# Layer 1 and layer 2 of an expert network on TensorE: one by one, or in pairs

## What is computed

```python
# block 1: gated recurrence along the sequence
g = sigmoid(norm(x) @ Wg.T + bg);  h = scan(h * (1 - g) + g * norm(x))
x = x + norm(h @ Wo.T + bo)
# block 2: top-1 of 8 experts, 320 places each, 2-layer networks 256 -> 1024 -> 256
eid = argmax(softmax(norm(x) @ router_w + router_b)); rank = place in the expert's queue
y = relu(buf @ w1 + b1) @ w2 + b2                       # for tokens with rank < 320
yov = relu(norm(x) @ ow1 + ob1) @ ow2 + ob2             # for all the others
x = x + norm(y or yov)
```

## Time and profile before

| | us |
|---|---|
| median of 3 runs | 1175.66 (1174.62 to 1176.27) |
| profiled execution | 1174.9 |
| its span | 1173.2 |
| PE busy | 1142.9 (97%) |
| DVE busy | 995.6 (85%) |
| ACT busy | 743.6 (63%) |
| POOL busy | 691.4 (59%) |

### The profile page before, as it was taken

One profiled execution on the slowest core, in us unless ns is written; L12 is line 12 of the kernel. 1 busy time (PEld: TensorE's weight loads), 2 busy tenths in 40 slices (PEclk: granted clock), 3 DMA queues, 4 the chain that ended last, 5 costly groups with the idle time before them and its releaser, 6 DMA issues.

```text
span 1173.2 us, 24398 instructions
## 1 busy us (share of the span) xinstructions
PE 1142.9 (97%) x7539; PEld 1018.6 (87%) x7539; DVE 995.6 (85%) x2737; ACT 743.6 (63%) x1379; POOL 691.4 (59%) x792
## 2 busy tenths in 40 slices
PE   7789999999999999999999999999999999999996
PEld 4578889888898888898888888889988888899996
DVE  6868888888889898988888888888898987778885
ACT  5356666566666666666656665666666667678783
POOL 4447667566665656566666665666656664414544
PEclk9999999999999999999999999999999999999998
DMA  9131111111111111110100111111111100245430
GB/s 262 37 100 55 37 51 48 43 38 36 36 36 36 36 36 36 36 36 18 36 23 31 36 36 36 36 36 36 36 36 36 36 18 19 86 141 182 147 132 34
DMA packets 59428, 65.09 MB, mean 55 GB/s; under 512 B 7835, under 2 KB 55629, under 8 KB 59268
## 3 DMA queue, kind: packets, MB, share of 16 engines
q1 hardware_dynamic: 52228, 59.36, 15.6%
q0 software_dynamic: 7168, 5.34, 1.5%
HBM read 40.19 MB, written 38.76 MB: 67 GB/s over the span
## 4 chain that ended last, share of the span: by engine, by line
PE 89%; DVE 4%; POOL 3%; ACT 2%; issue 2%; DMA 0%; DVEq 0%; POOLq 0%; ACTq 0%
PE psY L1426 12%; PE psY L1429 11%; PE psY L1428 11%; PE psH L1320 11%; PE psH L1322 11%; PE psH L1321 10%; PE psA L1320 5%; PE psA L1321 5%; PE psA L1322 5%; PE psT L1376 3%; PE psT L1333 2%; DVE st L858 1%; PE psT L1389 1%; PE psT L1391 1%; POOL rstd L399 1%
## 5 line engine op out<-in xcount | busy, mean ns | idle before, releaser
L620 ACT ACTIVATE hid<-psH,biasT 128x512 f32<-128x512 f32 (+1 forms) x312 | 202.7, 650 | 217.4 <-PE psH L1322 216.4
L1426 PE MATMUL psY<-W_hi,hid_hi 128*128 128x256 f32 x1168 | 336.6, 288 | 0.8 <-DVE hid_lo L1011 0.8
L1429 PE MATMUL psY<-W_hi,hid_lo 128*128 128x256 f32 x1168 | 329.6, 282 | 0.0
L1428 PE MATMUL psY<-W_lo,hid_hi 128*128 128x256 f32 x1168 | 328.9, 282 | 0.0
L399 POOL TENSOR_TENSOR rstd<-veps,mhalf 128x4 f32<-128x4 f32 (+2 forms) x103 | 142.0, 1379 | 169.1 <-DVE nmean L870 169.1
L1011 DVE TENSOR_TENSOR hid_lo<-hid,hid_hi 128x512 fp32r<-128x512 f32 (+1 forms) x308 | 201.0, 664 | 44.4 <-ACT hid_hi L625 39.3
L1320 PE MATMUL psH<-xfT_hi,W_hi 128*128 128x512 f32 (+1 forms) x624 | 235.4, 377 | 0.3 <-ACT hid L620 0.2
L1322 PE MATMUL psH<-xfT_hi,W_lo 128*128 128x512 f32 (+1 forms) x624 | 235.5, 377 | 0.0
L1321 PE MATMUL psH<-xfT_lo,W_hi 128*128 128x512 f32 (+1 forms) x624 | 234.6, 376 | 0.0
L1426 PEld LDWEIGHTS psY<-W_hi,hid_hi 128*128 128x128 f32 x1168 | 220.0, 188 | 10.8 <-DVE hid_lo L1011 1.9
L1428 PEld LDWEIGHTS psY<-W_lo,hid_hi 128*128 128x128 f32 x1168 | 220.2, 189 | 6.4
(11 more groups left out here) (172 smaller groups left out, 2181.9 us busy)
## 6 DMA issues: line engine op xcount, KB each, us to landing
xin<-L_attn_x SPq DMA_DIRECT2D x32, 512.0 KB, 3.5
stage<-L_ffn_w SPq DMA_DIRECT2D x16, 1024.0 KB, 5.6
out<-outt SPq DMA_DIRECT2D x31, 512.0 KB, 2.8
xbuf<-zrow SPq DMA_DIRECT2D x1, 2590.0 KB, 15.8
xin<-xbuf SPq DMA_DIRECT2D x8, 259.0 KB, 5.0
stage<-L_ffn_ow SPq DMA_DIRECT2D x2, 1024.0 KB, 8.0
xbuf<-x,idx POOLq DMA_INDIRECT x128
b_b<-L_ffn_b SPq DMA_DIRECT2D x1, 1024.0 KB, 6.4
```

The lines of the kernel that those rows point to most:

```text
L620: act.activation(hid[j % 2][:, at:n], psH[:, j % 2, at:n], ACT.Relu, bias=bias).then_inc(s_hid, 1)
L1426: pe.matmul(dst, hi, w[0][:, j, :], start=(j == 0 and (tail or t % 2 == 0)), stop=False, skip_group_check=True)
L1428: pe.matmul(dst, hi, w[1][:, j, :], start=False, stop=False, skip_group_check=True)
L1429: last = pe.matmul(dst, lo_, w[0][:, j, :], start=False, stop=(j == HC - 1), skip_group_check=True)
```

## The change

Parts stand in pairs. In a steady step the order behind `project` is now `layer1(2)`, `layer1(3)`, `transposes0(far)`, `rank(now)`, `layer2(0)`, `layer2(1)`, `layer1(4)`, `layer1(5)`, `layer2(2)`, `layer2(3)`, `gate(far)`, `layer1(6)`, `layer1(7)`, `layer2(4)`, `layer2(5)`, `transposes1(nxt)`, `layer2(6)`, `layer2(7)`. In an expert: `layer1(0)` to `layer1(3)`, `layer2(0)`, `layer2(1)`, and so on by two, with `transposes1(nxt)` behind `layer2(5)` instead of ahead of it. The number of instructions, their sizes and the programs of the other engines are the same.

```diff
-                for j in range(2, HC):
+                for j in range(2, HC, 2):
                     if run:
                         layer1(now, j, GT, W1[1])
+                        layer1(now, j + 1, GT, W1[1])
                         if j == 2:
                             pe.wait_ge(s_y, cnt(now, 2, 0))
-                    if j == 3 and ahead:
+                    if j == 2 and ahead:
                         transposes0(far)
                     if run:
-                        if j == (3 if up else 2):
+                        if j == 2:
                             rank(now)
                         layer2(now, j - 2, TG, W2[1])
-                    if j == 5 and ahead:
+                        layer2(now, j - 1, TG, W2[1])
+                    if j == 4 and ahead:
                         gate(far)
...
-                for j in range(HC + 2):
+                for j in range(0, HC + 2, 2):
                     if j < HC:
                         layer1(now, j, C, W1[u], EL1)
-                    if j == HC - 1 and live(nxt, E):
+                        layer1(now, j + 1, C, W1[u], EL1)
+                    if j == HC:
                         transposes1(nxt, ET, NG)
                     if j >= 2:
                         if j == 2:
                             pe.wait_ge(s_y, cnt(now, 2, 0) + 2 * NG)
                             pe.wait_ge(s_we_lo, cnt(now, 8, 8))
                         layer2(now, j - 2, ET, W2[u], EL1)
+                        layer2(now, j - 1, ET, W2[u], EL1)
```

## The result

The changed kernel takes 1186.6 us (median of four runs, 1185.7 to 1187.5) against 1176.0 us before in the same comparison: ratio 1.0089, 95% interval 1.0076 to 1.0102. It is slower, by 10.6 us where 38 were forecast.

A forecast was written before the change was run, and what follows sets the result against it. PE's queue was taken as the bound, with no slack in the chain through POOL's `tok`. Span 1173.2 + 36.5 (steady steps) + 2.8 (experts) = 1212.5, plus 1.7 and 0.8 = 1215.0, stated as 1214; range 1186 to 1218.

The forecast's parts named there:

- T0: PE's `transposes0(far)` in a steady step (L1333), which needs POOL's `tok`.
- PE reaches T0 at E + 9.46: Steady step: with `layer2(0)` moved behind it, PE comes to T0 at E + 9.46 instead of E + 10.92.
- E: The start of a step's `layer1(now, 0)` on PE, from which times within the step are counted, in us.
- Quiet step: Step with DVE's `result` at E + 0.20: T0 at E + 9.84, a stall of 0.38 us, +0.29 a step.
- Late step: Step with `veps` held beside `hst_lo`, `result` at E + 1.83: T0 at E + 10.90, stall 1.44 us, +1.35 a step.
- So I take every step as late: Steady loop: `hst_lo` still starts 0.05 us ahead of `veps` in every step, 27 x 1.35 = 36.5 us; chance 0.44.
- all steps quiet: Rival, steady loop: `veps` always ahead of `hst_lo`, 27 x 0.29 = 8 us, time 1184 to 1192; chance 0.13.
- What `veps` waits for: Late step: DVE's `veps` and POOL's `hst_lo` block each other; `veps` takes 2.54 us instead of 0.17.
- no hold at all: Rival, steady steps: `tok` ends at E + 9.20, before PE needs it, time 1173 to 1177; chance 0.04.
- The pairing saves 0.09 a step: PE, steady steps: fewer changes between `layer1` and `layer2` save some 0.03 us for each of three pairs.
- The experts: Seven experts: waits at `layer1(3)` for ACT's ReLU and at `layer2(5)` for `hid_lo`, 0.4 us each, 2.8 us.
- The clock: Rival: the new stall lowers PE's clock in each step, 46 us more, 1260; 0.10 together with any other stall.

The follow-up runs named there:

- t0_behind: The changed kernel with the experts of before and, in steady steps, `transposes0` and `rank` behind `layer2(0)` again; 1177.6 us, ratio 1.0012.
- late_hid_lo: `steady_only` with DVE's first `hid_lo` of a step held until POOL has made the deviation; 1210.6 us, ratio 1.0289.
- pad_long: `steady_only` with a POOL memset of 1280 bfloat16 columns between the scatters and `hst_lo` in each step; 1205.5 us, ratio 1.0249.
- steady_only: The changed kernel with the experts put back as before, pairs in the steady steps alone; 1185.9 us, ratio 1.0080.
- both_repairs: The steady steps of `t0_behind`, and experts in pairs with `transposes1` ahead of `layer2(5)`; 1182.3 us, ratio 1.0047.
- experts_only: The changed kernel with the steady steps put back as before, pairs in the experts alone; 1180.8 us, ratio 1.0037.
- after_again: The changed kernel, unchanged, measured once more; 1190.2 us, ratio 1.0117.

## Why the prediction was off

- *What bounds the kernel, and which wait grows:* right. The chain through POOL's `tok` to T0 is where the loop's loss lies; with T0 put back (`t0_behind`) it is gone.
- *PE reaches T0 at E + 9.46:* right, E + 9.47 where nothing held it. *Quiet step, T0 at E + 9.84:* measured E + 9.80. *Late step, E + 10.90:* measured 10.4 to 10.8 in `late_hid_lo`, 10.5 in `pad_long`. The price of a late step was sound: `late_hid_lo`, with 27 of them, is 24.7 us slower than `steady_only`, at 1210.6, beside the 1214 forecast (its experts are those of before).
- ***"So I take every step as late"* is the step that failed.** It took the 36.5 us of the sum where 5.9 (in the other execution 9.9) were lost. It had `hst_lo` at `gate` + 11.36 and `veps` at `gate` + 11.41, and argued that this distance holds because PE's stretch from `gate` to `transposes1` keeps its contents. After the change `gate` starts at 657.69 with E = 638.28, `hst_lo` at 668.50 = `gate` + 10.81, `veps` at 669.13 = `gate` + 11.44. `veps` stayed, since it does follow PE. `hst_lo` didn't: its place comes from POOL's scatters, and they start behind POOL's work on `nxt` (L437), which started at E + 19.36 before (651.64 - 632.28) and starts at E + 19.32 (657.60 - 638.28) now. It goes by E, not by `gate`, which moved from E + 19.08 to E + 19.41: PE's hold of 0.33 at T0 comes between, and gives POOL the lead that makes the next step not late. The rows of before, to be laid beside the 657.60 and 662.79 above:
```profile
651.64 1.42 POOL L437 TENSOR_TENSOR x<-veps,mhalf 128x4 f32<-128x4 f32 x1 [5.68 <-DVE nmean L870]
...
656.95 1.81 POOL L421 DMA_INDIRECT xbuf<-x,idx  x1 [0.17 <-issue]
```
  Scatters began 5.59 us behind `gate` and now begin 5.10; the four took 5.77 us to the last one's end (662.72) and take 5.42, as the first isn't stretched. That is 0.84 us; of it 0.29 is lost again to `hst_hi`, 0.55 is left. The forecast knew that 0.05 us decided, and took both times as fixed to within less than it had shown. `both_repairs`, which has the pairs and no hold, shows the other side: in a step with E = 666.88 `hst_lo` is 0.18 us ahead of `veps`, and `veps` takes its 2.39 us as before.
```profile
666.00 2.54 POOL L461 TENSOR_TENSOR hst_lo<-hst,hst_hi 128x512 fp32r<-128x512 f32 x2
...
666.18 2.39 DVE L869 TENSOR_SCALAR veps<-mv 128x4 f32<-128x4 f32 x1
```
  Both signs of being wrong that the forecast named came: T0 ahead of E + 9.8, and `veps` short.
- *What fits by luck:* 1186.6 us lies at the edge of the stated range, and in that of the rival "all steps quiet" (1184 to 1192), and PE's wait for `tok`, 10.5 us, is near the 10 named for that case. But about half of the steps were quiet, not all; the loop lost 5.9 us, not 8, the experts 4.0, not 2.8, and the 10.5 us come from 16 waits, not 27.
- *What `veps` waits for:* half right. It was taken as all or nothing, by who comes first. In the traces of all these kernels `veps` waits for both instructions of `hst_lo` when it starts up to 0.55 us behind the first (2.04 us in the step with 0.55), and only for the first at 0.62 or 0.63 (0.68 to 0.71 us); nothing in between was met. That "the two block each other" isn't shown: `hst_lo` took 2.55 us beside `veps` and 2.57 without. The Trainium skill, page "SBUF — State Buffer", section "SBUF: two separate sides", says of a DVE instruction in a mode that uses two ports, and of one with two inputs in SBUF beside a GpSimd instruction that reads SBUF, that whichever of it and the GpSimd instruction starts first gets their shared ports for its whole length, and the other blocks. Whether `veps`, with one input in SBUF, ran in such a mode, no trace tells. The 0.69 us agree with that rule; the 2.13, over the end of an instruction, it doesn't explain.
- *The rival "no hold at all":* it was given 0.04, and it is what happens in every second step. `tok` ended at E + 8.94, ahead of PE at 9.46; the short chain from the statistics (673.63 to 678.77) took 5.14 us, under the 5.38 priced. What was held against it, "DVE's `hid_lo` right behind stands as before", doesn't hold in the steps where a gap of 0.33 us stands ahead of that `hid_lo`. These were the late steps of before, so the 5.38 us priced for them held that gap already. `late_hid_lo` showed that it is that neighbourhood. So the rivals were right one by one, and what was wrong was to give each of them the whole loop: the result is a quiet step and an unheld one in turn, 31.55 and 31.17 us.
- *The pairing saves 0.09 a step:* it saves nothing. From T0 to the next E PE takes 701.00 - 679.30 = 21.70 us; before, 20.26 and `layer2(0)`'s 1.43 make 21.69. By the Trainium skill, page "TensorE: Matmul & The Clock Gate", section "Back-to-back issue gap", quoted in the forecast, nothing would be saved, and this trace agrees in that; its N/2.4 + 2.5 ns, which the section gives for a matmul by itself and not for a stream with weight loads, is 216 ns where the forecast's row has 232.
- *The experts:* 4.0 us were lost in the experts where 2.8 were forecast (`experts_only`: 0.56 each, not 0.4). The wait at `layer1(3)` was there, with about its size (0.45 us behind PE, 0.51 forecast), and wasn't the cause alone: `layer2(5)` with the transposes behind it, and `layer1(7)`, each hold an expert nearly as long when the others are away.
- *The clock:* it stayed up in the loop, as forecast. The granted clock was 1.00 over the whole loop, as before; the page shows 9 in every slice of PEclk but the last.

In the sum: 36.5 + 2.8 were forecast on the span; between the two profiled executions the loop and the experts gave 5.9 + 4.0.

## What to carry over

When two steps of a loop alternate, price each kind and carry the order through several steps, hold included: a stall on the bounding engine gives its suppliers time, so the next step starts from another phase. Where a few hundredths decide between cases, find out for each of the two events what it is tied to before taking their distance as fixed. When one wait is removed and nothing is won, look for a second that is as long behind it, and judge by the step, not by the total.

## What the runs showed of the hardware that I had not expected

- The start of DVE's `result` (PSUM and SBUF in, SBUF out) depended on something that isn't in the kernel. `t0_behind` and `both_repairs` have the same steady steps. With the last scatter ending 0.72 us behind E, `result` started at E + 1.60 in the first; with it ending at E + 0.74, at E + 0.20 in the second, which ran on another chip. POOL's last scatter and DVE's `result` in the one and in the other, where the first's E is 758.88 and the second's 760.62:
```profile
758.62 0.97 POOL L421 DMA_INDIRECT xbuf<-x,idx  x1 [0.30 <-issue]
...
760.48 1.29 DVE L1025 TENSOR_TENSOR ysb<-psY,ob_b 128x512 f32<-128x512 f32 x2 [2.15 <-PE psY L1429]
...
760.38 0.98 POOL L421 DMA_INDIRECT xbuf<-x,idx  x1 [0.30 <-issue]
...
760.82 1.29 DVE L1025 TENSOR_TENSOR ysb<-psY,ob_b 128x512 f32<-128x512 f32 x2 [0.74 <-PE psY L1429]
```
  In all eight traces of one chip and both of another `result` began 0.8 to 1.0 us behind the end of the last scatter in nearly every step where that ended behind E; the exceptions are the first step of the loop and a few steps where the scatter ended at E + 0.4 to E + 0.6 and `result` began at E + 0.3 to E + 0.4. In the four traces of a third chip and in the first of either kernel it began at E + 0.20 in the same steps. The rows name PE's matmul as the releaser in both. What delays it stays open, and that it goes by the chip is read from sixteen traces, not tested. The two medians of the changed kernel with and without it differ by 3.6 us; the kernel before, where T0 has the slack, loses nothing.
- A DVE instruction of 0.17 us (`veps`) took 3.40 us beside three of POOL's (a memset and two of `hst_lo`), and POOL's L399 took 1.42 us instead of 1.04 when DVE's `hid_lo` had begun first. L401 took 0.69 instead of 0.20 in such steps of the first trace, but 0.20 in those of `after_again`, where `hid_lo` began first as well.
